# A fused graph-attention and mixture-of-experts kernel: register addresses worked out one product ahead, scatters seven tiles behind, sums waited for by tile

## The reference

```python
x = x + gnn(layernorm(x), edges, weight, attn_l, attn_r)      # one gathered source row per token, softmax over 4 heads
t = layernorm(x)
probs = softmax(t @ router_w.T)                                # 8 experts
rw, re = top_k(probs, 2); rw = rw / rw.sum(-1)
out = t
for e in range(8):
    h = gelu(t @ w1[e] + b1[e])
    out = out + combine[:, e:e+1] * (h @ w2[e] + b2[e])
x = x + out
```

## Time and profile before

| | us |
|---|---|
| median of 3 runs | 480.43 (478.54 to 484.5) |
| the profiled execution | 482.3 |
| its span, first to last instruction | 480.6 |
| TensorE busy in the span | 397.2 (83%) |
| VectorE busy | 359.0 (75%) |
| ScalarE busy | 282.8 (59%) |
| GpSimd busy | 238.6 (50%) |

### The profile page before, as it was taken

How to read it: one execution, slowest core, us unless ns; L and a number is a source line. 1 busy time by engine, 2 the same in 40 slices (tenths; PEclk the granted TensorE clock), 3 DMA queues, 4 the chain that set the end, 5 groups by cost and what they waited for, 6 DMA issues and landing times.

```text
span 480.6 us, 11940 instructions
## 1 busy us (share of the span) xinstructions
PE 397.2 (83%) x3546; PEld 338.0 (70%) x3546; DVE 359.0 (75%) x1260; ACT 282.8 (59%) x743; POOL 238.6 (50%) x239
## 2 busy tenths in 40 slices
PE   5937989899989836344999999899999999898890
PEld 3837888788988825233888778677778887687770
DVE  4535999999899997793788777677677777677660
ACT  3434564646465569360767776666767776665760
POOL 7775787868686000004455524636455554643522
PEclk9987997979797955555899999999999999999996
DMA  4395526775848231102233211212132222222210
GB/s 149 113 234 157 156 76 189 191 223 150 247 112 250 46 123 79 66 16 51 75 81 82 69 37 59 79 58 81 57 92 69 79 71 57 79 64 64 69 46 20
DMA packets 18337, 48.27 MB, mean 100 GB/s; under 512 B 4719, under 2 KB 9354, under 8 KB 18276
## 3 DMA queue, kind: packets, MB, share of 16 engines
q0 software_dynamic: 10896, 29.61, 21.6%
q1 hardware_dynamic: 6626, 17.32, 12.3%
q10 hardware_dynamic: 756, 0.58, 0.4%
HBM read 34.42 MB, written 13.07 MB: 99 GB/s over the span
## 4 chain that ended last, share of the span: by engine, by line
PE 45%; DVE 18%; DMA 15%; ACT 7%; POOL 7%; issue 6%; DVEq 1%; ACTq 0%; POOLq 0%
PE bank L1359 14%; PE bank L1369 11%; DMA work<-token_table,order 8%; DMA acc<-in_x_dram,index 6%; PE bank L1225 5%; PE bank L1249 4%; POOL acc L469 4%; PE bank L1351 3%; PE bank L1366 2%; PE bank L1216 2%; POOL out_dram L511 2%; DVE acc L1171 2%; PE bank L1239 2%; PE bank L1228 2%; DVE work L1077 1%
## 5 line engine op out<-in xcount | busy, mean ns | idle before, releaser
L469 POOL DMA_INDIRECT acc<-in_x_dram,index x98 | 110.4, 1126 | 40.5 <-issue 23.5
L502 POOL DMA_INDIRECT work<-token_table,order x76 | 74.0, 974 | 105.7 <-DVE order L1108 65.9
L1359 PE MATMUL bank<-work,w_hi 128*128 128x128 f16 x1000 | 117.5, 224 | 0.3
L1359 PE MATMUL bank<-work,w_lo 128*128 128x128 f16 x500 | 104.1, 221 | 0.0
L676 ACT ACTIVATE h<-bank,b_col 128x128 f32<-128x128 f32 x250 | 77.5, 360 | 37.0 <-PE bank L1359 35.8
L511 POOL DMA_INDIRECT out_dram<-acc,order x49 | 50.4, 1028 | 88.4 <-DVE acc L1171 54.4
L1171 DVE SCALAR_TENSOR_TENSOR acc<-bank,work,acc 128x256 f32<-128x256 f32 (+1 forms) x125 | 60.4, 483 | 45.2 <-DVE acc L1152 19.6
L1359 PEld LDWEIGHTS bank<-work,w_hi 128*128 (+1 forms) x1000 | 67.1, 98 | 24.6 <-issue 3.2
L1369 PE MATMUL bank<-w_hi,h_hi 128*128 (+1 forms) x250 | 68.2, 273 | 0.0
L1369 PE MATMUL bank<-w_hi,h_lo 128*128 (+1 forms) x250 | 68.1, 272 | 0.0
L1369 PE MATMUL bank<-w_lo,h_hi 128*128 (+1 forms) x250 | 68.1, 272 | 0.0
(11 more groups left out here) (201 smaller groups left out, 731.6 us busy)
## 6 DMA issues: line engine op xcount, KB each, us to landing
token_table<-row_out SPq DMA_DIRECT2D x7, 931.0 KB, 4.8
acc<-in_x_dram SPq DMA_DIRECT2D x7, 784.0 KB
work<-in_L_ffn_w_dram SPq DMA_DIRECT2D x16, 256.0 KB, 5.3
acc<-in_x_dram,index POOLq DMA_INDIRECT x98, 3.7
work<-token_table,order POOLq DMA_INDIRECT x76, 2.9
out_dram<-acc,order POOLq DMA_INDIRECT x49, 2.5
acc<-in_x_dram SPq DMA_DIRECT2D x7, 105.0 KB
w_raw<-in_L_gnn_weight_dram ACTq DMA_DIRECT2D x1, 256.0 KB, 4.1
```

Of the source, the lines that this page charges most:

```text
L469: nc.gpsimd.indirect_dma_start(out=xds[:, t % RING, n, :], out_offset=None, in_=x, in_offset=bass.IndirectOffsetOnAxis(ap=index[:, n, t:t ...
L502: nc.gpsimd.indirect_dma_start(out=rows[:, k % ROWS_RING, :], out_offset=None, in_=table, in_offset=bass.IndirectOffsetOnAxis(ap=order[:, ...
L1359: last = nc.tensor.matmul(bank[i % RINGS][:, f * P:(f + 1) * P], first_of(hi, c, f), x2T[:, r, half, c * P:(c + 1) * P], start=(m == 0), s ...
```

## The change

Three things. `SCATTER_LAG` goes from 5 to 7. On TensorE, ScalarE and VectorE the addresses that depend on a run-time expert are asked for earlier: `lower_ap` puts the register instructions for an address at the place where it stands, and the later use of the same address finds the register. ScalarE and VectorE do it just before the wait of the instruction that uses it, TensorE one product ahead: those of `first` for the next item between the matmuls of `second`, and four of the five of `second` between the matmuls of the `first` ahead of it. And VectorE's `add_rows` and `accumulate` wait for the last sum of the same tile (and for the sums of the extras) in place of all sums before; the extras and `add_normal` wait as before.

```diff
--- before.py
+++ after.py
@@ -74,7 +74,7 @@
 ITEMS = [(k, None) for k in range(EXTRAS)] + [(EXTRAS + q, n) for q in range(TILES) for n in range(2)]
 ROWS_RING = 8
 X2_RING = 4
-SCATTER_LAG = 5
+SCATTER_LAG = 7
 
 PACK = 4
 WORDS = -(-TILES // PACK)
@@ -671,6 +671,8 @@
                 nc.scalar.activation(x2T[:, k % X2_RING, 0, :], bank[6 + k % 2][:, 0:D], ACT.Copy, scale=SPLIT).then_inc(s_sx_hi, 1)
 
             def hidden(i, bias_of):
+                for f in range(KT):
+                    nc.scalar.lower_ap(bias_of(f))
                 act.wait_ge(s_h, i + 1)
                 for f in range(KT):
                     last = nc.scalar.activation(h32[:, i % RINGS, f * P:(f + 1) * P], bank[i % RINGS][:, f * P:(f + 1) * P], ACT.Gelu,
@@ -1109,6 +1111,7 @@
 
 
             sums = Chain(dve, s_acc)
+            last_sum = {}
             experts, tiles = {}, {}
 
             def load_experts():
@@ -1143,13 +1146,14 @@
 
             def add_rows(k):
                 q = k - EXTRAS
-                sums.ready()
+                at_least(dve, s_acc, min(sums.n, SUMS[EXTRAS - 1]))
                 sums(nc.vector.tensor_tensor(acc[:, q, :], acc[:, q, :], rows[:, k % ROWS_RING, 0:D], ALU.add))
 
             def add_normal(k):
                 q = k - EXTRAS
                 sums.ready()
                 sums(nc.vector.tensor_tensor(acc[:, q, :], acc[:, q, :], x2[:, k % X2_RING, :], ALU.add))
+                last_sum[q] = sums.n
 
             def hidden_lo(i):
                 dve.wait_ge(s_hhi, i + 1)
@@ -1166,10 +1170,15 @@
                 else:
                     to = acc[:, k - EXTRAS, :]
                     weight_of = row[:, bass.ds(experts[k - EXTRAS][n] + COMB, 1)]
+                for ap in (weight_of, to):
+                    nc.vector.lower_ap(ap)
                 dve.wait_ge(s_y, i + 1)
-                sums.ready()
+
+                at_least(dve, s_acc, sums.n if n is None else max(SUMS[EXTRAS - 1], last_sum[k - EXTRAS]))
                 sums(nc.vector.scalar_tensor_tensor(out=to, in0=bank[RINGS + i % RINGS][:, 0:D], scalar=weight_of, in1=to,
                                                     op0=ALU.mult, op1=ALU.add))
+                if n is not None:
+                    last_sum[k - EXTRAS] = sums.n
                 assert sums.n == SUMS[i], (i, sums.n, SUMS[i])
 
             for k in range(4):
@@ -1351,22 +1360,58 @@
                     last = nc.tensor.transpose(bank[6 + k % 2][:, c * P:(c + 1) * P], x2[:, k % X2_RING, c * P:(c + 1) * P], ident[:])
                 last.then_inc(s_back, 1)
 
-            def first(i, first_of):
+            def first_weights(i, lo, c, f):
+                k, n = ITEMS[i]
+                w = (w_lo if lo else w_hi)[0]
+                if n is None:
+                    return w[:, NEW[k + 1], c, f * P:(f + 1) * P]
+                return w[:, bass.ds(experts[k - EXTRAS][n], 1), c, f * P:(f + 1) * P].rearrange("p e n -> p (e n)")
+
+            def second_weights(i, lo, c):
+                k, n = ITEMS[i]
+                w = (w_lo if lo else w_hi)[1]
+                if n is None:
+                    return w[:, NEW[k + 1], c, :]
+                return w[:, bass.ds(experts[k - EXTRAS][n], 1), c, :].rearrange("p e n -> p (e n)")
+
+            def second_bias(i):
+                k, n = ITEMS[i]
+                if n is None:
+                    return b2_parts[:, NEW[k + 1], :]
+                return b2_parts[:, bass.ds(experts[k - EXTRAS][n], 1), :].rearrange("p e n -> p (e n)")
+
+            FIRST_AT = [(lo, c, f) for f in range(KT) for c in range(KT) for lo in range(2)]
+            SECOND_AT = [None] + [(lo, c) for c in range(KT) for lo in range(2)]
+
+            def address(ap, kept_in_array):
+
+                nc.tensor.lower_ap(ap, for_matmul_weights=kept_in_array)
+
+            def first(i, j):
+
                 r = ITEMS[i][0] % X2_RING
                 for f in range(KT):
-                    parts = [(hi, half, c) for c in range(KT) for hi, half in ((0, 0), (0, 1), (1, 0))]
-                    for m, (hi, half, c) in enumerate(parts):
-                        last = nc.tensor.matmul(bank[i % RINGS][:, f * P:(f + 1) * P], first_of(hi, c, f), x2T[:, r, half, c * P:(c + 1) * P],
-                                                start=(m == 0), stop=(m == len(parts) - 1))
+                    parts = [(lo, half, c) for c in range(KT) for lo, half in ((0, 0), (0, 1), (1, 0))]
+                    for m, (lo, half, c) in enumerate(parts):
+                        last = nc.tensor.matmul(bank[i % RINGS][:, f * P:(f + 1) * P], first_weights(i, lo, c, f),
+                                                x2T[:, r, half, c * P:(c + 1) * P], start=(m == 0), stop=(m == len(parts) - 1))
+                        if m % 3 == 1 and j >= 0 and ITEMS[j][1] is not None:
+                            at = SECOND_AT[2 * f + m // 3]
+                            address(second_bias(j) if at is None else second_weights(j, *at), False)
                 last.then_inc(s_h, 1)
 
-            def second(i, second_of, bias_of):
+            def second(i, j):
+
                 pe.wait_ge(s_hlo, i + 1)
                 y = bank[RINGS + i % RINGS][:, 0:D]
-                nc.tensor.matmul(y, eights[:], bias_of(), start=True, stop=False)
+                nc.tensor.matmul(y, eights[:], second_bias(i), start=True, stop=False)
                 parts = [(h, lo, c) for c in range(KT) for h, lo in ((h_hi, 0), (h_hi, 1), (h_lo, 0))]
                 for m, (h, lo, c) in enumerate(parts):
-                    last = nc.tensor.matmul(y, h[:, i % RINGS, c * P:(c + 1) * P], second_of(lo, c), start=False, stop=(m == len(parts) - 1))
+                    if j < len(ITEMS) and ITEMS[j][1] is not None:
+                        for at in FIRST_AT[m + m // 5:m + 1 + (m + 1) // 5 + (m == 5)]:
+                            address(first_weights(j, *at), True)
+                    last = nc.tensor.matmul(y, h[:, i % RINGS, c * P:(c + 1) * P], second_weights(i, lo, c),
+                                            start=False, stop=(m == len(parts) - 1))
                 last.then_inc(s_y, 1)
 
             experts = {}
@@ -1387,20 +1432,10 @@
                 k, n = ITEMS[i]
                 if n != 1:
                     pe.wait_ge(s_sx_lo, k + 1)
-                if n is None:
-                    first(i, lambda lo, c, f: (w_lo if lo else w_hi)[0][:, NEW[k + 1], c, f * P:(f + 1) * P])
-                else:
-                    e = experts[k - EXTRAS][n]
-                    first(i, lambda lo, c, f: (w_lo if lo else w_hi)[0][:, bass.ds(e, 1), c, f * P:(f + 1) * P].rearrange("p e n -> p (e n)"))
+                first(i, i - LAG)
 
             def second_item(i):
-                k, n = ITEMS[i]
-                if n is None:
-                    second(i, lambda lo, c: (w_lo if lo else w_hi)[1][:, NEW[k + 1], c, :], lambda: b2_parts[:, NEW[k + 1], :])
-                else:
-                    e = experts[k - EXTRAS][n]
-                    second(i, lambda lo, c: (w_lo if lo else w_hi)[1][:, bass.ds(e, 1), c, :].rearrange("p e n -> p (e n)"),
-                           lambda: b2_parts[:, bass.ds(e, 1), :].rearrange("p e n -> p (e n)"))
+                second(i, i + LAG + 1)
 
             for k in range(2):
                 sorted_transpose(k)
```

## The result

The changed kernel took 467.12 us, the median of four executions (461.95 to 470.55), and the kernel before 480.26 us beside it (478.54 to 484.5). The ratio is 0.968, with a 95% interval of 0.961 to 0.975. The forecast was 469.0 us, within 457 to 477.5.

A forecast was written before the change was run, and what follows sets the result against it. TensorE, waiting for its own instructions, was taken to bound the sorted tiles at 3.60 us, with scatters next at 3.65. Gains of 11.1 + 0.5 = 11.6 us from 480.43 gave 469 us, range 457 to 477.5.

The forecast's parts named there:

- The chain of scatters as the next bound: Sorted tiles: each scatter awaits the landing before it, 2.85 + 0.8 = 3.65 us a tile, 175.2 us against 186.3.
- The share of late landings is kept: Scatters in sorted tiles: 14 of 49 landings over 3 us stay late, since instruction fetches don't change with the lag.
- Part 1: GpSimd's queue: lag seven frees gathers two tiles, some 7 us, earlier; ScalarE's waits go, which cost TensorE 9.9 to 13.5 us.
- rival (b): GpSimd's queue: gathers stay late because a slow scatter still stands ahead of a gather; 477 to 481 us, chance 0.15.
- the 11.1 us: Sorted tiles: the most the chain of scatters allows the change to gain, 186.3 us down to 175.2.
- rival (a): Sorted tiles: TensorE's issue stays the bound at 3.60 us, 3.72 with uneven scatters; 472.7 us, chance 0.23 together with (e).
- Part 2: TensorE's addresses worked out during the product ahead: sorted tile from 3.60 to 3.1-3.3 us; gain between 0 and 23.5 us.
- Part 3: ScalarE and VectorE: most of VectorE's 17.8 us idle goes, hidden in sorted tiles; 0.5 us gained between extras and tiles.
- Signs to look for: Profile after: scatters 3.6-3.7 us apart, landing waits over 60 us, gathered-row waits below 10, sorted first products 0.67-0.75 us.
- (c): Scatters land near 2.4 us throughout, so TensorE, VectorE and ScalarE together bound at about 3.3 us; 452 us, chance 0.09.
- (d): TensorE idles about 0.5 us a tile and loses its clock; fifteen such tiles would give 508 us; chance 0.05.
- (e): Early addresses are not kept and are worked out again; time that of rival (a), chance 0.23 together.

The follow-up runs named there:

- the six experiments: Six one-scatter-in-flight variants of before or after: lag or TensorE addresses alone; after without lag, TensorE addresses, or ScalarE/VectorE part; after with more fetches. Ratios 0.978 to 0.997.
- The added fetches of the experiment: Changed kernel plus 3000 already satisfied wait instructions on SyncE, idle after its last store: 468.38 us, ratio 0.984 to the kernel before.

## Why the prediction was right, and where its reasons were not

The time and the verdict were right: 11.6 us of gain forecast, 13.1 measured between medians. The bound that was to come next was right too. Which part of the change removes the old one was not, and two terms of the sum were off in opposite directions, which is luck. By its steps:

- **The bound before** (TensorE waits for its own instructions, 3.60 us a tile, 3.11 possible): right. With the scatters freed, the kernel before runs at 3.600 and the changed one at 3.05.
- **The chain of scatters as the next bound** (2.85 + 0.8 us): right, and it decided the result. The changed kernel starts 47 of 48 scatters 0.77 to 0.96 us behind a landing; two matmuls fewer don't move it; two scatters in flight do, by 26 us of median (0.921 against 0.968). The gap of 0.8 us was too small: I read it off the tail, and over all 48 steps it is 0.89 us, 42.9 us in all and not 38.3. By this the trace of before allowed the chain a gain of 6.1 us, not 11.1.
- **The share of late landings is kept, "the fetches come with the instructions":** mis-sized as well. I took 14 of 49 from one execution, and in the other profiles of these two chips it is 7 to 13; 8 in the changed one. The first 48 landings took 127.0 us where I had 136.9, and 129.0 to 133.4 us in the six experiments. The landings 9.9 us too high and the gaps 4.6 us too low left 175.2 us for the sum against 169.9 in the trace of after, its quickest execution; with landings of about 132 us the two errors nearly cancel. The cause named there is supported by a count over eight profiles, 384 scatters: of the 96 landings over 2.8 us, 86 had an instruction fetch of 16 kB running between 1.6 and 2.35 us after the scatter's start; of the 288 others 15 had. And in all of these the 15th of a scatter's 16 completions came by 2.9 us; only the last was late. One row of it: the scatter at 421.13 us of after met a fetch at 422.72; 30 of its 32 large packets started by 423.18, the other two at 424.04 and 424.47. I chose the stretch of 1.6 to 2.35 us after seeing the landings, and a count shows that the two go together, not more. The added fetches of the experiment, on the other queue, did not prove it, so the cause is likely and not shown.
- **Part 1, the waits for gathered rows go:** right for the lag alone, wrong in the changed kernel, where 27.0 us are left. I had the ring of buffers give two tiles of store and forgot what fills it: TensorE at 3.1 us a tile empties the store that scatters at 3.5 refill, since each gather stands behind a scatter. With TensorE at its old 3.60 us these waits are 1.6 us in all, and with the scatters freed their row is gone. That was rival (b)'s mechanism; it cost the chain of scatters nothing.
- **Which part gives the 11.1 us:** wrong. I booked all of it to the lag (part 1) and called TensorE's addresses secondary. The lag alone gave 0.997 and TensorE's part 0.988 alone, 0.024 as the last one added. What the runs showed in its place is that no part alone gives the gain and that the addresses carry more than the lag, whose own share stays within the intervals. With two bounds at 3.60 and 3.65 us the removal of either yields little; my own sum had both numbers and I read only the upper one as the gate, though rival (a) had the mechanism of the lag alone (3.72 us a tile there, 3.68 in its trace; the time fell less than it said).
- **Part 2, a tile near 3.1 us:** right (3.09 and 3.05), but not for the reason given. The bounds were "hidden" or "moved, not removed". It is also removed. The order of one sorted item's instructions in TensorE's stream, second product and first product, before and after (MATMUL rows of a first product shortened to their count):

```
before  pack, bias, reg, 1, reg, 1, 1, reg, 1, reg, 1, 1,
        reg, reg, pack, 2, reg, 1, pack, 2, reg, 1, pack, 2, reg, 1, pack, 2, reg, 1     15 register instructions
after   bias, reg, reg, pack, 1, reg, 1, pack, 1, reg, 1, pack, 1, pack, 1,
        2, pack, 1, 2, reg, 1, 2, reg, 1, 2, reg, 1                                      12 register instructions
```

  In the records of single instructions of before, which the views leave out, the median from one register instruction to the next is 0.11 us behind a single one and 0.12 us behind a pack, whether one matmul stands between them or two. 15 of them are 1.65 to 1.8 us an item, more than the 1.56 us of its matmuls (half a tile of 3.11); 12 are 1.32 to 1.44, less. By this estimate the issue was the bound before, and the array is after, which the paces of 3.60 and 3.05 us with freed scatters bear out. No run tells apart what fewer register instructions and what their new places give. The whole kernel has 11551 instructions in place of 11940.
- **Part 3:** the 17.8 us of VectorE went as said. In the sorted tiles it was hidden, as said: the traces with and without it differ there by their landings alone. The 0.5 us ahead of the first scatter was too little: 2 to 3 us. The two pairs of ratios have 1 to 2% in all for this part, more than these 2 to 3 us; the rest is open.
- **Signs to look for:** starts 3.54 us apart against 3.6 to 3.7; first products at 0.67, as said; the landing's row at 20.1 and not over 60, because the view gives most of those waits to the sums. TensorE is busy 97% of the stretch from 300 to 400 us and not near 85%, and the clock fell once.
- **Rivals:** (c), 452 us with quick landings, priced the other engines at 3.3 us together; they allow 3.05, and 441 us. (d) happened once, behind 2.66 us of idle time, and cost the chain nothing. (e) did not: the register instructions fell from 15 to 12.

The Trainium skill (Runtime: NRT & Kernel Launch, Instruction fetch mechanics) says that instructions are fetched in 16 KiB blocks and that this is mostly hidden. The traces agree on the size (20 packets, 0.33 MB in the earlier trace rows), though another queue carries 14 fetches of 8 kB in the same stretch. In the kernel with two scatters in flight TensorE was busy 50.00 of 50.00 us while seven such fetches of 16 kB ran, so they were hidden from it; by the count above they are probably not hidden from the scatters.

## What to carry to other kernels

Before tuning engines, look for a DMA that waits for the landing of its own predecessor: landing plus some 0.9 us, times the number of them, is a floor of the stage that no busy share shows, and two semaphores in turn remove it (26 us of 467 here). Count register instructions between matmuls against the matmuls' own time, and place them so that several are worked out together. Where two bounds lie within a few per cent of each other, test the parts of a change in pairs too: alone each is worth little here (0.997 and 0.988), and the last one in seems to be worth most of the whole (0.992 to 0.968). And take landings from more than one execution: here the same 48 took 127 to 137 us.

## What the runs showed of the hardware that was not expected

- On TensorE 0.11 to 0.12 us pass from one register instruction to the next, single or pack, with one or two matmuls between. A first product of 12 matmuls took 0.79 to 0.93 us with ten of them in its stream and 0.67 with four.
- One of a scatter's 16 completions tends to be late when a 16 kB instruction fetch runs beside it: 86 of 96 late landings, 15 of 288 others.
- An indirect DMA of GpSimd started 0.77 to 0.96 us after the landing that released it in 47 of 48 places of the changed kernel's trace, and once 3.22 us after it. The name in the view may be that of the other semaphore.
- The granted clock fell to its lower level for one tile of the changed kernel, after TensorE had been idle for 2.66 us; the 12 matmuls then took 1.28 us in place of 0.67.
- Matmuls in 50 us tell a bound better than busy time: 49.95 us busy were 553 matmuls in one kernel and 50.00 us were 652 in another, both at full granted clock.
- The third chip took 508.64 us for the kernel that takes 480 us elsewhere, with the loss partly before the stage studied; no run here says why.
